# An attention and spiking-MLP layer: products in two 64-row halves around the scores, and a new order of the MLP steps

## What is computed

```
xn  = layernorm(x)
Q, K, V = xn @ Wq.T + bq, xn @ Wk.T + bk, xn @ Wv.T + bv     # 16 heads of 16
Q, K    = rope(Q), rope(K)
attn    = softmax(causal(Q @ K.T / 4)) @ V                    # per head
h   = square(relu(xn @ W_fc.T))                               # 1,024 hidden features
y   = h @ W_proj.T
spk = (number of spikes of a 5-step leaky neuron driven by y) / 5
out = x + (attn @ Wo.T + bo) + spk
```

## Time and profile before

| | us |
|---|---|
| median of 3 runs | 2239.6 |
| lowest, highest | 2238.24, 2243.39 |
| the profiled execution | 2244.92 |
| its span | 2243.2 |
| PE busy | 2156.2 |
| PEld (weight loads) busy | 1406.2 |
| DVE busy | 1441.2 |
| ACT busy | 1437.5 |
| POOL busy | 1097.5 |

### The profile page before, as it was taken

One profiled execution on the slowest core, in us unless ns is written; L12 is line 12 of the kernel. 1 busy time (PEld: TensorE's weight loads), 2 busy tenths in 40 slices (PEclk: granted clock), 3 DMA queues, 4 the chain that ended last, 5 costly groups with the idle time before them and its releaser, 6 DMA issues.

```text
span 2243.2 us, 48570 instructions
## 1 busy us (share of the span) xinstructions
PE 2156.2 (96%) x16276; PEld 1406.2 (63%) x16276; DVE 1441.2 (64%) x2134; ACT 1437.5 (64%) x1673; POOL 1097.5 (49%) x1074
## 2 busy tenths in 40 slices
PE   3799999999999999999999999999999999989995
PEld 2656666666666666666666666666666666656653
DVE  5646566766757676566757667676676757646543
ACT  2376766667576675766667576665757667666663
POOL 4455454554645455453545545455464545535431
PEclk9899999999999999999999999999999999999998
DMA  3352544536345353644536354453634635345433
GB/s 137 110 175 88 157 130 115 182 87 197 101 127 168 97 184 88 173 115 132 174 84 192 101 143 144 113 185 84 188 106 120 181 91 181 92 133 155 109 97 94
DMA packets 169785, 298.89 MB, mean 133 GB/s; under 512 B 25089, under 2 KB 114945, under 8 KB 157185
## 3 DMA queue, kind: packets, MB, share of 16 engines
q1 hardware_dynamic: 169600, 296.10, 45.8%
HBM read 174.89 MB, written 103.28 MB: 124 GB/s over the span
## 4 chain that ended last, share of the span: by engine, by line
PE 83%; DVE 6%; ACT 4%; issue 4%; DMA 1%; POOL 1%; SPq 0%; ACTq 0%; DVEq 0%; POOLq 0%
PE pair L1068 33%; PE pair L1264 20%; PE pair L1228 15%; PE pair L1247 15%; ACT probs L708 2%; DVE count L928 2%; DVE stats L792 1%; ACT xT_hi L673 1%; PE pair L1155 1%; DVE h_sq L913 1%; DVE denom L852 1%; ACT h_sq L699 1%; PE pair L1080 1%; DVE numer L951 1%; POOL rot L599 0%
## 5 line engine op out<-in xcount | busy, mean ns | idle before, releaser
L708 ACT ACTIVATE probs<-pair 128x1024 f32<-128x1024 f32 x1152 | 1117.9, 1026 | 490.3 <-PE pair L1247 482.8
L617 POOL TENSOR_SCALAR_AFFINE_SELECT probs<-probs 128x512 f32<-128x512 f32 x512 | 375.0, 752 | 484.8 <-ACT probs L708 484.8
L609 POOL TENSOR_TENSOR h_lo<-h_sq,h_hi 128x512 fp32r<-128x512 f32 x256 | 383.9, 1500 | 437.4 <-DVE h_hi L915 436.9
L1264 PE MATMUL pair<-probs,v_sb 128*17 128x512 f32 (+3 forms) x6144 | 546.9, 489 | 6.1 <-DVE numer L951 5.2
L1247 PE MATMUL pair<-q_ring,k_ring 64*128 64x512 f32 (+3 forms) x3072 | 440.7, 381 | 16.8 <-ACT probs L708 13.7
L913 DVE TENSOR_TENSOR h_sq<-h_sq 128x512 f32<-128x512 f32 x256 | 201.3, 786 | 352.2 <-ACT h_sq L699 352.2
L1247 PEld LDWEIGHTS pair<-q_ring,k_ring 64*128 64x128 f32 x3072 | 227.3, 185 | 272.6 <-ACT probs L708 172.7
L1264 PEld LDWEIGHTS pair<-probs,v_sb 128*17 128x17 f32 x6144 | 152.3, 97 | 297.7 <-issue 264.1
L928 DVE SCALAR_TENSOR_TENSOR count<-y_sb,count 128x512 bf16<-128x512 f32 x256 | 294.1, 1149 | 6.8
L1228 PE MATMUL pair<-wproj_hi,h_hi 128*128 128x256 f32 x1024 | 293.0, 286 | 1.3 <-POOL h_lo L609 1.3
L1228 PE MATMUL pair<-wproj_lo,h_hi 128*128 128x256 f32 x1024 | 289.6, 283 | 0.0
(11 more groups left out here) (89 smaller groups left out, 2592.4 us busy)
## 6 DMA issues: line engine op xcount, KB each, us to landing
q_ring<-qk_dram SPq DMA_DIRECT2D x384, 128.0 KB
k_ring<-qk_dram SPq DMA_DIRECT2D x384, 128.0 KB
qk_dram<-planes SPq DMA_DIRECT2D x64, 512.0 KB, 2.8
qk_dram<-rot_b SPq DMA_DIRECT2D x64, 512.0 KB, 3.9
xn<-in_x SPq DMA_DIRECT2D x17, 1024.0 KB, 7.0
rs<-in_x SPq DMA_DIRECT2D x64, 256.0 KB, 2.7
acc_dram<-rs SPq DMA_DIRECT2D x64, 256.0 KB, 4.5
attn<-numer SPq DMA_DIRECT2D x256, 64.0 KB, 2.3
```

What stands on the lines that cost most here:

```text
L609: pool.tensor_tensor(h_lo[i % HB][:, :], h_sq[i % HB][:, :], h_hi[i % HB][:, :].bitcast(F32), ALU.subtract).then_inc(h_lo_done, 1)
L617: ins = pool.affine_select(view, view, [[0, 4], [1, P]], ALU.is_ge, 0.0, base=0, channel_multiplier=-1)
L708: act.activation(probs[BUFFER[n]][:, 2 * pr:2 * pr + 2, :], pair[m % NSLOT][:, :, :], ACT.Exp, scale=SCALE).then_inc(exp_done, 1)
L1264: ins = pe.matmul(pv_bank[32 * i:32 * i + VW, q0 - g * G:G], v_sb[:, kt, 4 * quad + i, :], probs[BUFFER[n]][:, i, at:at + width(kt, g)], s ...
```

## The change

Three kinds of thing change.

**Halves.** Q and K, V, and most expansions and contractions are no longer whole products. Two products are taken together, x and y. In the first half x is done on rows 0 to 63 and y on rows 64 to 127; in the second half the rows are swapped. Each bank so gets both parts of its sum, and x and y always write different banks. The first half stands ahead of the scores of unit 2n+1 (or 2n), the second behind them. The semaphores `qk_half`, `v_half`, `pair_half`, `mlp_half` and `mlp_part` tell PE that its own first half has ended. Pairs are: the even and odd bank of Q or K; two groups of V; two expansions; an expansion (6 x 512 columns) with a contraction (12 x 256 columns); the two banks of a contraction.

**Places.** V groups 0 and 1 stand around S of unit 1, groups 2 and 3 with both halves between S of units 2 and 3. The fourth transpose moves from behind S of unit 5 to between W and the first halves of step 2. Output products 0 to 2 move from behind the odd S to right behind W of steps 3 to 5; the fourth stays behind the odd S of step 6. The norms move in front of the odd S of step 7.

**MLP.** Expansions 0 and 1, 2 and 3 are pairs in steps 7 and 8, in four banks' turns (`fc_bank(i)`). From step 9 on an expansion and a contraction are a pair around the odd S; odd contractions stand alone in two halves around the even S of steps 10 to 16; expansions 6, 8, 11 and 13 stand alone as whole products between the even S and W; contraction 15 stands around the odd S of step 17. In intervals without attention everything is done whole. Tables for the first and last intervals are changed alike. The engines' `rectify`, `h_low` and `activate_h` follow the new order; `take_y` of the first half moves from step 12 to 13.

The core of the diff (tables and PE; the other engines follow the tables):

```diff
-V_AT = {0: (0, 1)}
-V_EARLY = {1: (2, 3)}
-T_AT = {1: (0, 1, 2), 2: (3,)}
-QK_AT = {2: ((0, 0), (0, 1)), 3: ((1, 0), (1, 1)), 4: ((2, 0), (2, 1)), 5: ((3, 0), (3, 1))}
-O_AT = {3: 0, 4: 1, 5: 2, 6: 3}
+V_MID, V_AT = {1: 2}, {0: 0}
+T_MID, T_AT = {2: (3,)}, {1: (0, 1, 2)}
+QK_AT = {2: 0, 3: 1, 4: 2, 5: 3}
+O_MID, O_AT, O_FINAL = {3: 0, 4: 1, 5: 2}, {6: 3}, {3: 0, 4: 1, 5: 2, 6: 3}
...
+MLP = ({10: 1, 11: 3, 12: 5, 13: 7, 14: 9, 15: 11, 16: 13}, {11: 6, 12: 8, 14: 11, 15: 13},
+       {7: ((0, 1), None), 8: ((2, 3), None), 9: ((4,), 0), 10: ((5,), 2), 11: ((7,), 4), 12: ((9,), 6), 13: ((10,), 8),
+        14: ((12,), 10), 15: ((14,), 12), 16: ((15,), 14), 17: ((), 15)})
...
-Y0_AT, Y1_AT, Y_FINAL_AT = 12, 17, 15
+Y0_AT, Y1_AT, Y_FINAL_AT = 13, 17, 14
...
+        def fc_bank(i):
+
+            return bank_b if i == 1 else bank_c if i == 3 else bank_a
...
+            def half(x, y, stage):
+                first, each = stage == FIRST_HALF, len(y) // len(x)
+                for_x, for_y = (slice(0, 64), slice(64, P)) if first else (slice(64, P), slice(0, 64))
+                for n, (to, w, rows, opens, closes) in enumerate(x):
+                    x_ins = pe.matmul(to, w[for_x, :], rows[for_x, :], start=opens and first, stop=closes and not first,
+                                      skip_group_check=True)
+                    for to, w, rows, opens, closes in y[each * n:each * n + each]:
+                        y_ins = pe.matmul(to, w[for_y, :], rows[for_y, :], start=opens and first,
+                                          stop=closes and not first, skip_group_check=True)
+                return x_ins, y_ins
...
+            def expand_contract(b, nb, item, i, c, first, final, stage):
...
+                elif stage == FIRST_HALF:
+                    ready_to_contract(b, item, c, first, final)
+                    pe.wait_ge(relu_done, item + i)
+                    if c % NFT:
+
+                        pe.wait_ge(proj_done, item + c)
+                    half(expand_parts(i), contract_parts(c, 0) + contract_parts(c, 1), stage)[1].then_inc(mlp_half, 1)
                 else:
+                    pe.wait_ge(mlp_half, halves_ahead(nb, c, final))
+                    parts = expand_parts(i)
+                    half(parts[:KD + 1], contract_parts(c, 1), stage)[1].then_inc(mlp_part, 1)
+                    one, other = half(parts[KD + 1:], contract_parts(c, 0), stage)
+                    one.then_inc(fc_ps, 1)
+                    other.then_inc(proj_done, 1)
...
                 for n in range(NSTEP):
+                    if (more or final) and n in around:
+                        contract(b, nb, item, around[n], True, first, final, ahead)
                     if att:
                         scores(b, 2 * n, last)
+                        if (more or final) and n in around:
+                            contract(b, nb, item, around[n], True, first, final, behind)
+                    if (more or final) and n in alone_at:
+                        expand(nb, item, alone_at[n], final)
                     if last and n == 0:
                         run(b - 1, LAST_RUN, last)
                     if att and n in RUN_AT:
                         run(b, RUN_AT[n], last)
...
+                    for m in T_MID.get(n, ()) if more or final else ():
+                        transpose(b, tb, m, att)
+                    if last and not final and n in O_MID:
+                        output(b - 1, O_MID[n], final)
+                    if more and n == NORM_AT and not first:
+                        norms(nb, norm_bank)
...
+                    if att and n in V_MID:
+                        values(b, V_MID[n], again, FIRST_HALF)
+                        values(b, V_MID[n], again, SECOND_HALF)
+                    if att and n in V_AT:
+                        values(b, V_AT[n], again, FIRST_HALF)
+                    if more and n in QK_AT:
...
+                        query_key(nb, QK_AT[n], tb, ahead)
+                    if (more or final) and n in beside:
+                        mlp(b, nb, item, *beside[n], last, first, final, ahead)
                     if att:
                         scores(b, 2 * n + 1, last)
-                    for m in V_AT.get(n, ()) if att else ():
-                        values(b, m, again)
+                        if n in V_AT:
+                            values(b, V_AT[n], again, SECOND_HALF)
+                        if more and n in QK_AT:
+                            query_key(nb, QK_AT[n], tb, behind)
+                        if (more or final) and n in beside:
+                            mlp(b, nb, item, *beside[n], last, first, final, behind)
                     for m in T_AT.get(n, ()) if more or final else ():
                         transpose(b, tb, m, att)
```

More of the change, by code:

```diff
@@ L111 @@
[L111 to L116, removed]
+FIRST_HALF, SECOND_HALF, WHOLE = range(3)
@@ L990, in interval @@
                             normalise(nb + 1, t)
+                    if more and n == Y0_AT:
+                        take_y(half_of(b, 0, first, final, again), item + NFT - 1)
                     if last and n == 0:
@@ L1097, in query_key @@
-                m = slice((2 * is_k + eo) * P, (2 * is_k + eo + 1) * P)
-                parts = [p for k in range(KD) for p in (
-                    (wqk_hi[:, k, m], xT_hi[:, k, cols]), (wqk_lo[:, k, m], xT_hi[:, k, cols]),
-                    (wqk_hi[:, k, m], xT_lo[:, k, cols]))]
-                split_product(qk_bank[u][eo], parts).then_inc(qk_ps, 1)
-            def values(b, n, again):
+                if stage == FIRST_HALF:
+                    half(even, odd, stage)[1].then_inc(qk_half, 1)
+                else:
+                    whole(even).then_inc(qk_ps, 1)
+                    whole(odd).then_inc(qk_ps, 1)
@@ new lines, in value_parts, with values @@
+            def value_parts(n):
+                return two_tiles(v_bank[n], [[p for k in range(KD) for p in (
+                    (xT_hi[:, k, t * P:(t + 1) * P], wv_hi[:, k, :]), (xT_hi[:, k, t * P:(t + 1) * P], wv_lo[:, k, :]),
+                    (xT_lo[:, k, t * P:(t + 1) * P], wv_hi[:, k, :]))] for t in (2 * n, 2 * n + 1)])
+            def values(b, n, again, stage):
+                if stage == SECOND_HALF:
+                    pe.wait_ge(v_half, b * 2 + n // 2 + 1)
+                    one, other = half(value_parts(n), value_parts(n + 1), stage)
+                    one.then_inc(v_ps, 1)
+                    other.then_inc(v_ps, 1)
+                    return
@@ L1118, in values @@
-                ins.then_inc(v_ps, 1)
-            def multiply_out(bank, b, n):
-                for a in range(2):
-                    t = 2 * n + a
-                    ins = split_product(bank[:, a * D:(a + 1) * D],
-                                        [(attn[:, k, t * P:(t + 1) * P], wo_sb[:, k, :]) for k in range(KD)])
-                ins.then_inc(wo_ps, 1)
-            def output(b, n, more, final):
+                half(value_parts(n), value_parts(n + 1), stage)[1].then_inc(v_half, 1)
@@ L1130, in output, with multiply_out @@
+            def multiply_out(bank, n):
+                whole(two_tiles(bank, [[(attn[:, k, t * P:(t + 1) * P], wo_sb[:, k, :]) for k in range(KD)]
+                                       for t in (2 * n, 2 * n + 1)])).then_inc(wo_ps, 1)
+            def output(b, n, final):
                 if n == 0:
```

289 lines of the change are left out of this document (161 added, 128 removed).

## The result

The changed kernel takes 2439.4 us (median of 4 runs, 2434.6 to 2441.0) against 2241.5 us of the kernel before in the same session: ratio 1.088 [1.085, 1.091], 198 us slower. The forecast was 92 us slower. The sign was right, the forecast rise is less than half of the measured one, and the time lies above the whole range. The profiled execution spans 2432.8 us.

The account below looks back on a forecast made before the run. PE, busy 96% of the span, was taken as the bound. Waits of 11.8 less 5.5 saved gave +6.3 us per interval, +92 in all: 2331 us; the forecast's own range 2295 to 2370, widened to 2205 to 2385.

Parts of the forecast that it names:

- Saving of 5.5: Per interval, 29 fewer changes between kinds of product on PE at 0.19 us each: 5.5 us saved.
- (a): Rival: the saving wins, DVE and POOL run ahead; -2.5 us per interval, some 2205 us; chance 0.17.
- (b): Rival: only PE's waits for ACT stay; +0.8 us per interval, 2250 us; chance 0.10.
- (c): Rival: halves are 10% slow when accumulating into two banks; +5.7 us per interval on top, some 2415 us; chance 0.07.
- (e): Rival: the halves aren't done two at a time, products double; over 3000 us; chance 0.01.
- Wait 1: Even scores behind odd ones wait for ACT's second exponential: 8 x 0.45 = 3.6 us, plus 1.1 behind step 17.
- Wait 2: V in step 1: second V pair waits, 0.7 us; V copies on ACT delay scores of unit 4, +0.57 us.
- Wait 3: First output product, moved right behind step 3's weighing, waits for DVE's division making attn: 3.05 us, range 0 to 3.7.
- Wait 4: Step 10: two contractions follow with no weighing between: 0.3 us.
- Wait 5: Contraction 11, ahead of the scores of unit 30, waits for h_lo: 1.9 us, 0.7 without the mask, 1.5 taken.
- Wait 6: Contraction 15, moved in front of the last scores, waits for h_lo: 1.0 us, range 0.6 to 1.3.
- Rival (d): Clock falls to the lower level behind the wait for attn; +2 us per interval, +28, 2360 us; chance 0.10.

Follow-up runs that it names:

- E5: Changed kernel with the second exponential of each odd run cut to half its columns from the second attention interval on (output wrong, timing only): 2360.5 us, ratio 1.051.
- E1: Changed kernel with PE's loop over intervals 1 to 13 written out, so PE never jumps back: 2401.8 us, ratio 1.070 to the kernel before.
- B1: Kernel before the change with PE's loop written out: 2248.8 against 2246.2 us, ratio 1.0016.
- H2: H1 with PE's loop written out: 2262.6 us, ratio 1.008 to the kernel before.
- H1: Changed kernel with halves only for pairs of steps 9 to 16, output products and fourth transpose behind odd runs, bias additions in step 14: 2298.3 us, ratio 1.023.
- E3: Changed kernel with every pair of halves a whole product again, pairs behind the odd run, odd contractions ahead of the even run: 2331.6 us, ratio 1.038.

## Why the prediction was right in sign and half in size

Point by point, per interval, forecast against the trace after:

- **Saving of 5.5.** The parts that can be read are as forecast: scores inside halves 0.45 to 0.53 us, halves at 0.12 and 0.23 per pair, and 44 changes of kind in one interval where the kernel before has 72 (73 and 44 were counted). The total was not measured by itself. Rivals (a), (b), (c) and (e) are out: no saving won, the waits 3, 5 and 6 came, the halves do not run slow, and pairs start together.
- **Wait 1, even runs, 3.6.** Six runs take 1.01 to 1.06 instead of 0.56, S2 0.93 instead of 0.47, and S6 0.34 more: 3.6. E5 shows that the exponential sets it. At step 17, 1.1 forecast: without a jump 2.92 against 1.75, so 1.2.
- **Wait 2, V and S4, 0.7 + 0.57.** 0.3 and 0.7. The wait for V0's copy, 0.36 of the first, doesn't come on top: it is a part of the 0.46 of S2 that wait 1 already has.
- **Wait 3, the first output product, 3.05.** 4.79 from the start of the weighing to the product less 1.84 of weighing: 2.95. The chain of rows was right. What followed was not in the sum: the product and the halves behind it at the lower clock, +1.8 in the mean.
- **Wait 4, step 10, 0.3.** 0.33.
- **Wait 5, contraction 11, 1.5.** 2.4, with 2.20 of idle. I had calculated 1.9 and taken 1.5, between the value with and without the mask; there was no reason to go below the calculation.
- **Wait 6, contraction 15, 1.0.** 1.13.

That is 12.6 for the waits that I had against 11.8. The rest of the interval's growth is what I did not have:

- **The jump.** 4.18 from S35 to the weighing in the mean where 2.92 stands without a jump: +1.3, and the weighing at the lower clock in 8 turns of 12, 3.9 instead of 2.27: +1.1. E1 prices it at 38 us, 2.9 per interval with what else changed. The forecast called the covered jump nothing, without saying so: B1 shows that it was nothing, before. The step that failed is the one about covers ("it is gone only at 3, 5 and 6"): it asked which engine's work was covered at each moved product, and not what PE's own instruction stream needed.
- **The clock.** Rival (d) had this at 0.10 and +28 (+2 per interval) for wait 3, and the forecast's sum had nothing. It came, at a chance too low for a wait of 3.05 beside one of 3.37 in the earlier trace rows: +1.8 behind attn. It also came where neither the sum nor the rival had it: behind the jump (above) and behind contraction 11, in 3 intervals of 12 at 1.5 each, +0.4.
- **Smaller waits:** contraction 8 for y_sb 0.7, S13 for exponentials that stand behind other ACT work 0.7, and four output products of 1.93 instead of 1.81 us, 0.5.

Sum: 12.6 + 1.3 + 1.1 + 1.8 + 0.4 + 1.9 = 19.1 of waits and lower clock; less 5.5 that is 13.6, against 12.6 measured (146.3 - 133.7). The surplus of 1.0 stays open; the 5.5 is a forecast, and a saving of 6.5 would close it. Of the 6.3 us by which the forecast was short per interval, 3.3 are the lower clock at three places, 1.3 the jump, 0.8 the waits that were in the sum and 1.9 the smaller ones, less that 1.0. What follows the twelve intervals came 28 us longer, in line with two more intervals at the measured rate and the forecast's +2.

What the forecast had as tests came out so: PE waiting for attn once (2.9), for h_lo twice (30 times in all), runs in halves 0.47 long. The interval of 139 to 140 did not come. PE is idle 11.5 us of the one shown, where some 10 were forecast, so the greater part of the miss is time in which PE is busy: 134.7 us, its slow stretches included, instead of some 130.

**Open.** What in the jump takes 2 to 3 us (the trace has no row for it); the 1.0 by which the sum is too large; and which idle time lowers the clock, as below.

## What to carry to other kernels

Cutting changes between kinds of product is worth 0.19 us each only while what stands between two dependent runs is still longer than what the engine that feeds them takes; here 29 changes were to pay 5.5 us, and the thinner cover cost more. Before moving work on a nearly full engine, list for each wait not only who is late but what the idle time itself triggers (the clock) and what else was covered at that place (the jump of the engine's loop): here the lower clock cost 1.8 us per interval behind attn, and the exposed jump 2.9 with the clock behind it. Where a chain of rows gives a number, take it, not a milder one.

## What the runs showed of the hardware

- **A loop's jump on PE can cost nothing or over 2 us; in these traces it costs where PE has waited shortly before it.** Before: no gain from writing the loop out (1.0016 [1.0004, 1.0029]). After: 38 us for 12 jumps (E1), 36 in the hybrid (H2 against H1), with 2.16 and 2.82 us of idle where a wait of 1.05 or even 0.40 us came shortly ahead of the jump, and with none in E3, where the same contraction did not wait. What happens in the jump no trace shows.
- **Short idle can lower the granted clock, and the length of the idle alone does not decide.** In the changed kernel the clock fell behind all 14 waits for attn (2.88 us of idle; means of 0.50 to 0.64 over the next 4 us), behind 8 of 12 jumps (1.95 to 2.58 us) and behind 4 of 15 waits at contraction 11 (2.17 to 2.20 us). In H1 it stayed up behind 4 of 12 jumps (2.33 to 2.47 us in those four), in E5 behind 4 of 14 waits for attn (2.80 us), and in E3 behind all 14 (1.57 to 1.63 us); yet in E3 it fell behind two idle stretches of 0.89 and 0.42 us with 0.5 us of scores between them, in 8 of twelve intervals. Three stretches of PE's windows show it, the first behind 1.99 us at a jump (965.00), the others behind 2.20 and 2.19 at contraction 11:

```profile
965.60:968.20 2.60, 2.60 (x30) 0.86 (x30) 0.12 (x1) 1.88 (x2) 0.55 (x1) 1.00 0.39 111
1084.40:1088.40 4.00, 4.00 (x38) 3.05 (x42) 3.90 (x5) 2.16 (x3) 3.38 (x3) 1.00 0.47 119
1522.91:1526.91 4.00, 4.00 (x30) 3.56 (x31) 3.90 (x5) 1.94 (x2) 3.36 (x3) 0.57 0.43 118
```

- **64-row halves that accumulate into two banks run at the pace of whole products**, 0.12 us per 256 columns and 0.23 per 512, with both loads hidden behind the first pair. Two halves of the array side by side lose nothing here in pace.
